# A two-layer graph network with experts on one Trainium2 core: three stages joined into one program per engine

## The chip, the cores and the metric

The kernel runs on one core of a Trainium2 chip. The metric is the device time of one execution in microseconds. Five instruction streams run beside each other: PE (TensorE), DVE (VectorE), ACT (ScalarE), POOL (GpSimd) and SP (SyncE), which here only issues DMAs. Streams wait for each other on semaphores. Gathers and scatters by an index (indirect DMAs) are issued by POOL alone.

## The reference, cut to what matters

12500 nodes of 256 numbers pass through four blocks, each added to x. All of them begin with a layer norm of x.

```python
x = x + L0_gnn(layernorm(x), edges)      # attention over 212500 edges, 4 heads
x = x + L0_ffn(layernorm(x))             # 8 experts of three layers, mixed by one softmax
x = x + L1_gnn(layernorm(x), edges)      # attention, 8 heads, then a layer norm with gains
x = x + L1_ffn(layernorm(x))             # this one has a router:
    # h = x @ W_gat (4 heads x 4 experts); attention over 131072 router edges gives scores
    # e = leaky_relu(a_src[src] + a_dst[dst]); softmax over the edges of one dst; agg = sum(alpha * h[src])
    # scores = layernorm(agg) averaged over heads; the top 2 of 4 experts, softmax over these two
    # out = sum over experts of gate * (gelu(x @ W1 + b1) @ W2 + b2)
```

The change is about the last two lines of x: the end of the second attention (L1_gnn), the experts of L1_ffn, and the attention over the router's edges.

## The kernel before, in words

Nodes stand in 98 blocks of 128 (node b * 128 + p on partition p). Everything is float32. The edges of both graphs are sorted by destination on the chip at the start. `gnn_two_layers` runs the stages one after another; each stage opens a `Ctx`, which holds its memory and semaphores, and a `Block` with one program for each engine. When a `Ctx` with semaphores closes, all engines meet at a barrier, the semaphores are cleared, and they meet again (L52).

The stages that matter here:

- **The message stage of the second attention** (`sum_messages`, tiles named g1sm). 1760 tiles of 128 edges, taken 32 at a time into two slots. POOL gathers the 128 source rows of a tile (L1276), DVE computes softmax weights and multiplies messages (L1529), PE adds the messages of one destination by a matrix of zeros and ones (L1384), DVE carries the running sums along (L1551), and SP writes them to `sums` in HBM. The gathers of a tile may start when PE has used the tile that stood in its place. At the start POOL issues 64 gathers, DVE prepares and waits for the first 32 of them by way of ACT (L1325) and PE (L1360).
- **The end of the second attention** (`finish_and_route`, tiles named g1fa). Blocks go in 49 pairs. POOL fetches the last running sum of each node of a pair (`Sums.fetch`, L1618, two indirect DMAs a pair, at most two pairs in flight), DVE divides by the sum of weights and takes part in two layer norms, ACT normalises and takes roots, PE transposes and multiplies by the router's weights. Results: the new x, the transposed normed rows `turned`, and the router's rows (24 numbers a node) in `keep`, which go to the table `rtab` in HBM. For each block POOL also scatters the destination's score to the first edge of each node in `rfill` (L1928). In POOL's program 24 pairs (`AHEAD`) are fetched first; then each pair n does the fetch of pair n + 24, if there is one, and the two scatters of pair n. At the end POOL waits until the table and all scatters are written.
- **The experts** (`expert_outputs`, tiles named f). 25 steps, 24 of four blocks and one of two. A step runs the four experts in turn: PE multiplies `turned` by W1 into four banks (L2590), ACT takes gelu (L2567), PE multiplies by W2 (L2607), DVE adds the bias (L2633), SP writes the output `z`. PE computes the hidden layer of the next expert before the outputs of the present one.
- **The sums over the router's edges** (`EdgeSums`, tiles named re), inside the experts' programs. Each partition has 1024 consecutive sorted edges; 22 groups of 46 and one of 12. `split_keys` (L748 to 785, 26 operations of DVE, each waiting for the one before) takes the sorted keys apart into source numbers (`src`), marks of a new destination (`first`) and what is needed to join the partitions. POOL's `fetch` (L799, L811) gathers one row of `rtab` for each edge column, 1024 in all, at most eight lots ahead of the experts' outputs. In step g + 3 DVE works on group g: `highs` (L846 to 865) after the second expert, `sums` (L876 to 885) after the fourth; ACT takes the exponents between them (L831), SP loads the scores of the destination (L819) and stores the rows to `rsum` (L825).
- **`finish`** (tiles named rf): group 22, and sums that go over the end of a partition are joined: two transposes on PE, short operations of DVE and ACT, one gather and one scatter on POOL.
- **`choose_and_sum`** (tiles named cs): the last stage.

Before the experts start there is a barrier at the end of `finish_and_route` and of the scope around it; then SP loads x and the keys, ACT copies the 98 x 24 node values to another place (L742), DVE splits the keys, and POOL waits for 18 of the 26 operations. Between the experts and `finish`, and after `finish`, there are barriers too.

Of the kernel before, what the change touches and what calls it, by code (L numbers as in the profile page):

```python
# [11 lines left out]
P = 128  # L12
# [20 lines left out]
HELD = 20  # L33
SPAN = 32
# [658 lines left out]
class EdgeSums:  # L693
# [4 lines left out]
    G, LAG = 46, 3  # L698

    def __init__(self, nc, K, c, cols, H, F, table, sorted_keys, start, count, nodes, made, fill, rsum, endi, has):  # L700
        self.nc, self.K, self.cols, self.H, self.table = nc, K, cols, H, table
        self.nodes, self.made = nodes, made
# [5 lines left out]
        assert self.REST > 0 and self.NG % 2 == 0  # L708
# [14 lines left out]
        (self.loaded, self.numbered, self.moved, self.ready, self.began_in, self.ad_in, self.piece, self.diff_ready,  # L723
         self.exp_ready, self.piece_done, self.kept) = (c.sem("re" + n) for n in (
             "loaded", "numbered", "moved", "ready", "began_in", "ad_in", "piece", "diff_ready", "exp_ready",
             "piece_done", "kept"))
        every = self.rows[:, :, :].rearrange("p c w -> p (c w)")
        spare = every[:, cols * X - 2 * (cols + 1):]
        self.dst, self.dstf = spare[:, 0:cols + 1].bitcast(I32), spare[:, cols + 1:2 * (cols + 1)]
        self.lone, self.run = spare[:, 0:cols], spare[:, cols + 1:2 * cols + 1]  # L730
        assert cols - -(-2 * (cols + 1) // X) >= 2 * self.G
# [13 lines left out]
    KEYS, SPLIT = 18, 26  # L745

    def split_keys(self, dve):
# [26 lines left out]
        assert link.n == self.KEYS  # L774
# [12 lines left out]

    def span(self, g):
        return (g * self.G, self.G if g < self.NG else self.REST)
# [3 lines left out]
    def fetch(self, pool, outputs):  # L793

        nc, G = self.nc, self.G
        nc.gpsimd.iota(self.base[:, :], [[0, 1]], base=0, channel_multiplier=self.cols).then_inc(self.numbered, 1)
        nc.gpsimd.iota(self.selfi[:, :], [[P, NB]], base=0, channel_multiplier=1).then_inc(self.numbered, 1)
        pool.wait_ge(self.ready, self.KEYS)
        nc.gpsimd.indirect_dma_start(self.began[:, :], None, self.table,  # L799
                                     bass.IndirectOffsetOnAxis(ap=self.head0[:, 0:1], axis=0)).then_inc(self.began_in, 16)  # L800
        for g in range(self.NG + 1):
            col, n = self.span(g)
            if g >= 2:
                pool.wait_ge(self.rows_in[g % 2], 16 * G * (g // 2))
            lots = [col + n * j // self.LOTS for j in range(self.LOTS)]
            for u in range(col, col + n):
# [4 lines left out]
                nc.gpsimd.indirect_dma_start(self.rows[:, u, :], None, self.table,  # L811
# [10 lines left out]
    def store(self, sp, g, col, n):  # L822

        sp.wait_ge(self.piece_done, g + 1)
        sp.dma_start(self.rsum.rearrange("(p c) w -> p c w", p=P)[:, bass.ds(col, n), :],  # L825
                     self.rows[:, bass.ds(col, n), :]).then_inc(self.kept, 16)
# [8 lines left out]
    def highs(self, dve, g, col, n, landed):  # L835
# [8 lines left out]
        high = lambda a, b: self.rows[:, bass.ds(col + a, b - a), W:X]  # L844
# [9 lines left out]
        link(tt(score, self.rows[:, bass.ds(col, n), 0:H], ad, ALU.add))  # L854
# [13 lines left out]
    def sums(self, dve, g, col, n):  # L868
# [5 lines left out]
        rows = lambda a, b, c, d: self.rows[:, bass.ds(col + a, b - a), c:d]  # L874
# [13 lines left out]
    def finish(self):  # L888
# [5 lines left out]
        with Ctx(nc, "rf") as c:  # L894
            turned = c.ps("turned", [P, 3, P])
            backp = c.ps("backp", [P, 2, W])
            wide = c.sb("wide", [P, 2, W])
            state = c.sb("state", [P, 3, P])
            high, total = c.sb("high", [P, P + 1]), c.sb("total", [P, P + 1])
            step = c.sb("step", [P, 2, P])  # L900
            met, join = c.sb("met", [P, X]), c.sb("join", [P, 3, W])
            merged = c.sb("merged", [P, X])
            (ch, spread, rows_turned, step_ready, step_exp, state_ready, back, met_in, join_ready, join_exp, merge_ready,
             merge_out) = (c.sem(q) for q in (
# [268 lines left out]
def sum_messages(nc, K, name, tiles, H, table, lay, sums, room, more, beside, landed, begun=0):  # L1173
# [10 lines left out]
    with Ctx(nc, name) as c:  # L1184
# [39 lines left out]
        with nc.Block() as block:  # L1224

            @block.sync
            def _(sp):
# [32 lines left out]
                if beside is not None:  # L1260
                    beside(sp)
# [1728 lines left out]
```

## Time and profile before

| | |
|---|---|
| median of 3 runs | 9239.54 us (9236.39 to 9247.44) |
| the profiled execution | 9238.97 us |
| its span, first to last instruction | 9237.2 us |
| busy in the span: PE, DVE, POOL, ACT | 75%, 69%, 56%, 36% |

A time in a row is counted in us from the start of the span. A row of a timeline has start, length, engine, line, operation, result and operands, and in brackets how long the engine was idle before it and what ended that. "issue" is idle time in which the engine waited for nothing that the profile shows; for POOL's indirect DMAs it is 0.3 us each. The rows of POOL's DMAs are the time that POOL works on the issue, not that of the transfer. A row of the table by stage has the stretch, its length, the busy time of PE, of its weight loads, of DVE, ACT and POOL with the number of instructions, the granted clock of PE as a share of 2.4 GHz, the share of the DMA engines, and GB/s.

### The profile page before, as it was taken

The page shows a single profiled execution, that of the slowest core. Times are in us where ns is not written, and L with a number is a line of the kernel's source. Part 1 is how long each engine was busy: PE and PEld are TensorE (multiplying, and loading weights), DVE is VectorE, ACT ScalarE, POOL GpSimd, SP SyncE. Part 2 cuts the span into 40 slices and gives each one's busy share as a digit, 9 for nine tenths or more (in the row PEclk, how much of TensorE's full clock was granted, in tenths as well). Part 3 has the DMA queues.
Part 4 walks back from the last instruction along what each step waited for, and adds up shares of the span by engine and source line. Part 5 has one row for each costly group of instructions (what it writes and reads, how often), then busy time and mean ns, then how long its engine had stood idle before and what let it go on. Part 6 is the DMA issues. An engine that isn't in the chain of part 4 may idle for free. (4 is left out here: it accounts for less than half of the span.)

```text
span 9237.2 us, 87312 instructions
## 1 busy us (share of the span) xinstructions
PE 6943.7 (75%) x21953; PEld 4016.8 (43%) x21953; DVE 6330.2 (69%) x18686; ACT 3346.2 (36%) x7429; POOL 5144.8 (56%) x5327
## 2 busy tenths in 40 slices
PE   1536666666668999999997677777777649999985
PEld 1422232222225555555555233333333346666665
DVE  9967777777778777787665788888888851322235
ACT  1324344434443333333334344444444452222224
POOL 0157777777771111011543777777777577777754
PEclk9868888888889999999998677777777659999997
DMA  3256776677661000000325677777677652222229
GB/s 121 68 164 219 223 222 217 219 222 223 217 220 54 28 28 28 19 28 31 27 24 161 201 224 225 220 225 226 219 224 225 207 173 54 73 71 69 67 64 340
DMA packets 672170, 1355.24 MB, mean 147 GB/s; under 512 B 203371, under 2 KB 401870, under 8 KB 670642
## 3 DMA queue, kind: packets, MB, share of 16 engines
q0 software_dynamic: 238688, 579.40, 24.2%
q1 hardware_dynamic: 406352, 744.60, 22.9%
q10 hardware_dynamic: 26626, 25.65, 0.8%
q8 instruction: 178, 2.92, 0.1%
q14 instruction: 326, 2.67, 0.1%
HBM read 712.31 MB, written 649.65 MB: 147 GB/s over the span
## 5 line engine op out<-in xcount | busy, mean ns | idle before, releaser
L1276 POOL DMA_INDIRECT g_acc<-htab,g1sm_src x1760 | 1687.6, 959 | 545.5 <-issue 495.0
L1276 POOL DMA_INDIRECT g_acc<-htab,g0sm_src x1740 | 1650.0, 948 | 541.7 <-issue 488.2
L1384 PE MATMUL g1sm_sump<-g_acc,g1sm_to 128*128 128x264 f32 x3520 | 1481.3, 530 | 355.1 <-DVE g_acc L1529 327.3
L1384 PE MATMUL g0sm_sump<-g_acc,g0sm_to 128*128 128x260 f32 x3520 | 1320.8, 476 | 268.6 <-DVE g_acc L1529 226.9
L811 POOL DMA_INDIRECT re_rerows<-rtab,re_resrc x1024 | 994.2, 971 | 312.1 <-issue 307.8
L1384 PEld LDWEIGHTS g1sm_sump<-g_acc,g1sm_to 128*128 128x128 f32 x3520 | 660.0, 233 | 1132.0 <-DVE g_acc L1529 778.1
L1384 PEld LDWEIGHTS g0sm_sump<-g_acc,g0sm_to 128*128 128x128 f32 x3520 | 593.7, 210 | 958.3 <-DVE g_acc L1529 649.7
L2213 POOL DMA_DIRECT2D x<-g_acc x25 | 20.0, 800 | 1490.6 <-DVEq L2448 1349.4
L2633 DVE TENSOR_TENSOR k_arena<-f_yp,k_arena 128x512 f32<-128x512 f32 x196 | 135.6, 692 | 966.7 <-PE f_yp L2607 966.7
L1529 DVE TENSOR_TENSOR g_acc<-g_acc,g1sm_weightp 128x256 f32<-128x256 f32 x1760 | 716.5, 407 | 67.1 <-ACT g1sm_weightp L1318 67.1
L1529 DVE TENSOR_TENSOR g_acc<-g_acc,g0sm_weightp 128x256 f32<-128x256 f32 x1760 | 717.6, 408 | 21.7 <-ACT g0sm_weightp L1318 21.7
L2344 PE MATMUL f_yp<-k_arena 128*128 128x256 f32 x3136 | 712.8, 380 | 12.9 <-DVE g_acc L2437 9.1
L2309 PE MATMUL f_h1p<-k_arena 128*128 128x512 f32 (+1 forms) x1600 | 708.6, 586 | 0.7 <-ACT k_arena L2265 0.7
L2309 PE MATMUL f_h2p<-k_arena 128*128 128x512 f32 (+1 forms) x1600 | 706.2, 584 | 0.9 <-ACT k_arena L2274 0.9
L2607 PE MATMUL f_yp<-k_arena 128*128 128x256 f32 x3136 | 693.3, 379 | 2.4 <-ACT k_arena L2567 2.4
L2344 PEld LDWEIGHTS f_yp<-k_arena 128*128 128x128 f32 x3136 | 594.4, 190 | 167.0 <-issue 79.4
L2437 DVE SCALAR_TENSOR_TENSOR g_acc<-f_yp,f_wgt,g_acc 128x256 f32<-128x256 f32 x784 | 342.5, 479 | 456.2 <-PE f_yp L2344 450.9
L2607 PEld LDWEIGHTS f_yp<-k_arena 128*128 128x128 f32 x3136 | 595.8, 190 | 124.3 <-issue 45.4
L2274 ACT ACTIVATE k_arena<-f_h2p,f_shift,f_scale 128x512 f32<-128x512 f32 (+1 forms) x400 | 304.6, 768 | 917.8 <-PE f_h2p L2309 917.8
L1305 ACT ACTIVATE g1sm_to<-k_iota,g1sm_side 128x128 f32<-128x128 f32 x1760 | 556.7, 386 | 116.7 <-PE g1sm_sump L1384 116.7
L1305 ACT ACTIVATE g0sm_to<-k_iota,g0sm_side 128x128 f32<-128x128 f32 x1760 | 556.8, 387 | 18.2 <-PE g0sm_sump L1384 17.3
L2567 ACT ACTIVATE k_arena<-f_hp,k_f1b1s 128x512 f32<-128x512 f32 (+1 forms) x400 | 264.3, 679 | 782.2 <-PE f_hp L2590 782.0
(462 smaller groups left out, 11199.1 us busy)
## 6 DMA issues: line engine op xcount, KB each, us to landing
sums<-k_arena SPq DMA_DIRECT2D x275, 528.0 KB
sums<-k_arena SPq DMA_DIRECT2D x220, 520.0 KB
sums<-g_acc SPq DMA_DIRECT2D x165, 528.0 KB, 4.4
sums<-g_acc SPq DMA_DIRECT2D x165, 520.0 KB, 4.2
z<-k_arena SPq DMA_DIRECT2D x96, 512.0 KB, 3.0
k_arena<-z SPq DMA_DIRECT2D x33, 1024.0 KB, 13.5
sums<-g0sm_now SPq DMA_DIRECT2D x55, 520.0 KB
g_acc<-htab,g1sm_src POOLq DMA_INDIRECT x1760
```

Of the source, the lines that this page charges most:

```text
L811: nc.gpsimd.indirect_dma_start(self.rows[:, u, :], None, self.table, bass.IndirectOffsetOnAxis(ap=self.src[:, u:u + 1], axis=0))\
L1276: nc.gpsimd.indirect_dma_start(slot[a][:, u, :], None, table, bass.IndirectOffsetOnAxis(ap=src[a][:, u:u + 1], axis=0)).then_inc(landed[a] ...
L1305: ab = nc.scalar.activation(to[s][:, u, :], K["iota"][:, :], ACT.Abs, bias=mark[a][:, q * LOT + u:q * LOT + u + 1])
L1384: nc.tensor.matmul(bank(k, u), to[u // LOT % RING][:, u % LOT, :], slot[a][:, u, 0:W], start=True, stop=True).then_inc(summed, 1)
L1529: tt(m, m, weight[:, u, :].unsqueeze(2).to_broadcast([P, H, D]), ALU.mult).then_inc(msg_ready, 1)
L2274: nc.scalar.activation(hs[e % 2][:, m, 0:J * P], pp[m][:, 0:J * P], ACT.Relu, bias=shift[:, l, e, m:m + 1], scale=scale[:, l, e, m:m + 1])\
L2309: mm = nc.tensor.matmul(pp[m][:, 0:J * P], ws[:, e, k, m * P:(m + 1) * P], rhs[:, k, 0:J * P], start=(k == 0), stop=(k == KC - 1))
L2344: mm = nc.tensor.matmul(yp[j // 2][:, j % 2, :], h2s[e % 2][:, k, j * P:(j + 1) * P], wos[:, e, k, :], start=(k == 0), stop=(k == KC - 1))
L2437: m = nc.vector.scalar_tensor_tensor(out=row, in0=yp[q][:, j % 2, :], scalar=wgt[:, j, e:e + 1], in1=row, op0=ALU.mult, op1=ALU.add)
L2567: nc.scalar.activation(hs[e % 2][:, m, 0:J * P], hp[m][:, 0:J * P], ACT.Gelu, bias=b1s[:, e, m:m + 1])\
L2607: mm = nc.tensor.matmul(yp[j // 2][:, j % 2, :], hs[e % 2][:, k, j * P:(j + 1) * P], w2s[:, e, k, :], start=(k == 0), stop=(k == HC - 1))
L2633: nc.vector.tensor_tensor(zs[e % 2][:, 2 * q:2 * q + 2, :], yp[q][:, :, :], b2s[:, e, :].unsqueeze(1).to_broadcast([P, 2, DIM]), ALU.add)\
```

## The change

The three programs of each engine (end of the attention, experts with the edges' sums, `finish`) are put one behind the other in a single `Block`; the barriers between them are gone, and semaphores order them. For this:

- `split_keys` and the load of its keys move to the start of the message stage (`sum_messages` has a new argument `keys`), on DVE ahead of the first tile's weights and on SP ahead of the load of the experts' weights; POOL's two iotas (`number`) stand ahead of its first gather.
- the running sums that are fetched keep 72 blocks instead of 80, and `AHEAD` is 36 pairs instead of 24.
- `keep` is now the place where the last stage reads the node values; ACT's copy is gone.
- the rows of the edges lie in the memory of the running sums, in a ring of ten groups; POOL waits for a group's store before the tenth group after it. Marks and source numbers lie in memory that the first layer's experts left.
- SP loads the experts' first rows of x halfway through the end of the attention. POOL no longer waits there for its scatters; SP does, after three steps of the experts. POOL waits for the table and for DVE's divisions, then gathers.
- PSUM is eight banks, shared by name: the transposes and the experts' outputs use banks 0 and 1, the router's products and `finish` 2 and 3, the hidden layers 4 to 7.

```diff
+KEPT = 72
-    G, LAG = 46, 3
+    G, LAG, RING = 46, 3, 10
...
-        self.src = c.sb("resrc", [P, cols], I32)
-        self.rows = c.sb("rerows", [P, cols, X])
-        self.first = c.sb("refirst", [P, cols])
+        self.src, self.first = marks[:, 0:cols].bitcast(I32), marks[:, cols:2 * cols]
+        self.rows = room[:, 0:self.RING * self.G * X].rearrange("p (c w) -> p c w", w=X)
...
-    def keep_nodes(self, act):
-        self.nc.scalar.copy(self.nodes, self.made).then_inc(self.moved, 1)
-        act.wait_ge(self.moved, 1)
+    def number(self, pool):
+        nc = self.nc
+        nc.gpsimd.iota(self.base[:, :], [[0, 1]], base=0, channel_multiplier=self.cols).then_inc(self.numbered, 1)
+        nc.gpsimd.iota(self.selfi[:, :], [[P, NB]], base=0, channel_multiplier=1).then_inc(self.numbered, 1)
...
+    def held(self, g):
+        return g % self.RING * self.G
...
     def fetch(self, pool, outputs):
-        nc.gpsimd.iota(self.base[:, :], [[0, 1]], base=0, channel_multiplier=self.cols).then_inc(self.numbered, 1)
-        nc.gpsimd.iota(self.selfi[:, :], [[P, NB]], base=0, channel_multiplier=1).then_inc(self.numbered, 1)
-        pool.wait_ge(self.ready, self.KEYS)
         nc.gpsimd.indirect_dma_start(self.began[:, :], None, self.table,
...
             if g >= 2:
                 pool.wait_ge(self.rows_in[g % 2], 16 * G * (g // 2))
+            if g >= self.RING:
+                pool.wait_ge(self.kept, 16 * (g - self.RING + 1))
...
-                nc.gpsimd.indirect_dma_start(self.rows[:, u, :], None, self.table,
+                nc.gpsimd.indirect_dma_start(self.rows[:, self.held(g) + u - col, :], None, self.table,
...
-def sum_messages(nc, K, name, tiles, H, table, lay, sums, room, more, beside, landed, begun=0):
+def sum_messages(nc, K, name, tiles, H, table, lay, sums, room, more, beside, landed, begun=0, keys=None):
...
-                if beside is not None:
-                    beside(sp)
+                if keys is not None:
+                    keys.load_keys(sp)
+                beside(sp)
...
+                if keys is not None:
+                    keys.number(pool)
...
                 dve.wait_ge(cleared, 3)
+                if keys is not None:
+                    keys.split_keys(dve)
                 for s in range(HEAD):
                     weigh(s, 0, 0, 0)
...
-    N, R, AHEAD, LATE, TURNED = NB // 2, 4, 24, 8, 7
+    N, R, LATE, TURNED = NB // 2, 4, 8, 7
-    KEPT = HELD * CHUNK // 2
+    PAIRS = AHEAD = KEPT // 2
...
+            if n == N // 2:
+                for q in range(CHUNK // 2):
+                    sp.wait_ge(xT_kept[q], 16)
+                ahead(sp)
         for s in range(R):
             sp.wait_ge(xT_kept[s], 16 * len(range(s, N, R)))
+        sp.wait_ge(done, N)
...
         pool.wait_ge(kept, 16 * N)
-        pool.wait_ge(placed, 16 * NB)
+        pool.wait_ge(divided, N)
...
         for i in range(LAG):
             step(i, CHUNK, CHUNK)
+        sp.wait_ge(placed, 16 * NB)
         edges.load(sp, 0, 0, G)
...
-                edges.keep_nodes(act)
-                edges.split_keys(dve)
...
-            acc = g.sb("acc", [P, HELD * CHUNK, DIM + heads[1]])
+                places = g.sb("acc", [P, KEPT * width])[:, :]
...
+                with nc.Block() as block:
+                    @block.gpsimd
+                    def _(pool):
+                        fa_pool(pool)
+                        ex_pool(pool)
+                        rf_pool(pool)
+                    @block.tensor
+                    def _(pe):
+                        fa_pe(pe)
+                        ex_pe(pe)
+                        rf_pe(pe)
+                    @block.vector
+                    def _(dve):
+                        fa_dve(dve)
+                        ex_dve(dve)
+                        rf_dve(dve)
...
```

SP and ACT are joined in the same way. What each engine computes is unchanged.

## Rows read from the trace of the kernel before

**Rows 1.** Table by stage: end of attention, seam, experts; columns as told above.
```profile
7407.00:7545.00 138.00, 74.99 (x340) 71.50 (x340) 103.14 (x437) 86.31 (x222) 108.12 (x99) 0.50 0.75 217
7571.00:7621.00 50.00, 0.14 (x1) 0.04 (x2) 0.14 (x2) 2.35 (x2) 27.00 (x30) 0.50 0.08 20
7621.00:8940.00 1319.00, 1318.98 (x4580) 871.31 (x4581) 356.20 (x1032) 322.91 (x448) 994.71 (x1025) 1.00 0.27 67
```

**Rows 2.** Groups by line: POOL's gathers of messages; busy, mean, idle before them.
```profile
L1276 POOL DMA_INDIRECT g_acc<-htab,g1sm_src x1760 | 1687.6, 959 | 545.5 <-issue 495.0 <-PE g1sm_sump L1384 40.8 <-DMA g1sm_src<-srcs 9.6
```

**Rows 3.** Waits in the experts' stage: us in total, times, longest.
```profile
POOL re_rerows L811 <- issue: 307.8, 1010, 0.3
```

**Rows 4.** Timeline, first expert matmul of PE and first edge gather of POOL.
```profile
7621.02 16.79 PE L2590 MATMUL f_hp<-k_arena 128*128 128x512 f32 x32 [49.87 <-DMA k_arena<-turned]
...
7634.53 0.96 POOL L811 DMA_INDIRECT re_rerows<-rtab,re_resrc  x1 [0.30 <-issue]
```

**Rows 5.** Timeline of POOL, end of the attention: fetches (L1618) and scatters (L1928).
```profile
7327.12 0.98 POOL L1618 DMA_INDIRECT g_acc<-sums,k_lasts  x1 [56.01 <-POOLq L52]
...
7366.49 1.01 POOL L1618 DMA_INDIRECT g_acc<-sums,k_lasts  x1 [1.30 <-DMA g_acc<-sums,k_lasts]
...
7406.66 1.29 POOL L1928 DMA_INDIRECT rfill<-k_arena,k_starti  x1 [0.31 <-issue]
...
7539.94 1.19 POOL L1618 DMA_INDIRECT g_acc<-sums,k_lasts  x1 [0.30 <-issue]
...
7604.95 0.98 POOL L1928 DMA_INDIRECT rfill<-k_arena,k_starti  x1 [0.30 <-issue]
```

**Rows 6.** Timeline of DVE, end of the attention: divisions 13 and 29, last reciprocal.
```profile
7377.23 0.69 DVE L2027 TENSOR_TENSOR g1fa_t<-g_acc,g1fa_rden 128x512 f32<-128x512 f32 x1
...
7437.15 0.69 DVE L2027 TENSOR_TENSOR g1fa_t<-g_acc,g1fa_rden 128x512 f32<-128x512 f32 x1
...
7545.02 0.25 DVE L2020 RECIPROCAL g1fa_rden<-g_acc 128x16 f32<-128x16 f32 x1 [3.93 <-DMA g_acc<-sums,k_lasts]
```

**Rows 7.** Timeline, start of the message stage: gathers 1 and 32, first use.
```profile
5047.65 1.02 POOL L1276 DMA_INDIRECT g_acc<-htab,g1sm_src  x1 [9.60 <-DMA g1sm_src<-srcs]
...
5086.52 0.95 POOL L1276 DMA_INDIRECT g_acc<-htab,g1sm_src  x1 [0.30 <-issue]
...
5089.32 1.05 ACT L1325 COPY g1sm_asrc<-g_acc 128x512 f32<-128x512 f32 x1 [56.24 <-DMA g_acc<-htab,g1sm_src]
...
5091.58 0.49 DVE L1433 SCALAR_TENSOR_TENSOR g1sm_fill<-g1sm_ends,g1sm_smallp 128x128 f32<-128x128 f32 x2 [40.20 <-PE g1sm_smallp L1360]
```

**Rows 8.** Timeline of DVE, the split of the keys: first, eighth, last long operation.
```profile
7623.54 0.69 DVE L756 TENSOR_SCALAR re_resrc<-re_rerows 128x1024 int32<-128x1024 int32 x1 [6.62 <-DMA re_rerows<-rsorted]
...
7630.23 1.22 DVE L764 TENSOR_REDUCE re_relead<-re_rerows 128x1 f32<-128x1024 f32 x1
...
7635.17 0.36 DVE L785 CAST r_endi<-re_retmpn 128x98 int32<-128x98 f32 x1
```

**Rows 9.** Timeline in the edges' layout, early on: a gather beside a wide operation.
```profile
528.23 2.28 DVE L1125 SCALAR_TENSOR_TENSOR k_arena<-k_arena 128x2048 f32<-128x2048 f32 x1
528.66 2.74 POOL L1053 DMA_INDIRECT g_acc<-htab,el_srcs  x1 [11.68 <-DVE el_srcs L1106]
```

**Rows 10.** Timeline at the end: group 21's last gather, first use, join, last stage.
```profile
8924.21 0.94 POOL L811 DMA_INDIRECT re_rerows<-rtab,re_resrc  x1 [0.30 <-issue]
...
8965.83 0.35 DVE L854 TENSOR_TENSOR re_rediff<-re_rerows,re_read 128x184 f32<-128x184 f32 x1
...
8985.59 0.17 DVE L846 TENSOR_SCALAR re_relow<-re_refirst 128x12 f32<-128x12 f32 x1 [2.13 <-PEq L52]
...
9006.86 0.34 SPq L2699 DMA_DIRECT2D cs_par<-in_L_ffn_b_gat_dram  x1
```

**Rows 11.** Table by stage: the experts' first microseconds, columns as in rows 1.
```profile
7621.00:7624.00 3.00, 2.98 (x4) 1.45 (x5) 0.46 (x1) 0.00 (x0) 0.00 (x0) 0.50 0.68 210
7627.00:7630.00 3.00, 3.00 (x9) 1.33 (x8) 2.93 (x3) 1.37 (x2) 0.00 (x0) 1.00 0.00 0
```

More of the change, by code:

```diff
@@ new lines, in finish, with sync @@
+        wide, join = parts[4].rearrange("p (q w) -> p q w", q=2), parts[6].rearrange("p (q w) -> p q w", q=3)
+        (ch, spread, rows_turned, step_ready, step_exp, state_ready, back, met_in, join_ready, join_exp, merge_ready,
+         merge_out) = (c.sem("rf" + q) for q in (
+             "ch", "spread", "rows_turned", "step_ready", "step_exp", "state_ready", "back", "met_in", "join_ready",
+             "join_exp", "merge_ready", "merge_out"))
+        def sync(sp):
+            self.store(sp, NG, col, n)
@@ new lines, in scalar, with tensor @@
+        def scalar(act):
+            self.weigh(act, NG, n)
+            act.wait_ge(step_ready, 1)
+            nc.scalar.activation(step[0:W, :, :], step[0:W, :, :], ACT.Exp).then_inc(step_exp, 1)
+            act.wait_ge(join_ready, 1)
+            nc.scalar.activation(join[:, 0:2, :], join[:, 0:2, :], ACT.Exp).then_inc(join_exp, 1)
+        def tensor(pe):
+            pe.wait_ge(spread, 1)
+            for q, t in enumerate((self.edge[:, 0:W], wide[:, 0, :], wide[:, 1, :])):
+                mm = nc.tensor.transpose(turned[0:W, q, :], t, K["ident"][:, :])
+            mm.then_inc(rows_turned, 1)
+            pe.wait_ge(state_ready, 1)
+            for q, t in enumerate((total, high)):
+                mm = nc.tensor.transpose(backp[:, q, :], t[0:W, 0:P], K["ident"][0:W, 0:W])
+            mm.then_inc(back, 1)
@@ L1842, in _, with finish_and_route @@
                     pool.wait_ge(stored[s], 16 * len(range(s, N, HS)))
-def finish_and_route(nc, K, name, acc, H, xin, xout, gamma, ws, table, keep, arena, sums, start, count, fill, starti, turned):
+def finish_and_route(nc, K, c, banks, acc, H, xin, xout, gamma, ws, table, keep, arena, sums, start, count, fill, starti, turned,
+                     ahead, placed):
     D = DIM // H
-    N, R, AHEAD, LATE, TURNED = NB // 2, 4, 24, 8, 7
+    N, R, LATE, TURNED = NB // 2, 4, 8, 7
     C, TW = ws.shape[2], table.shape[1]
@@ new lines, in gpsimd, with scalar, step @@
+    def gpsimd(pool):
+        assert edges.LOTS == 2 * NE and (edges.NG + 1) * edges.LOTS - 1 - edges.AHEAD <= (NCH - 1) * 2 * NE + LAST // 2 * NE
+        edges.fetch(pool, y_ready)
+    def scalar(act):
+        def step(i, J, g=None):
+            for e in range(NE):
+                for m in range(HC):
+                    act.wait_ge(h_ready, i * (NE * HC) + e * HC + m + 1)
+                    nc.scalar.activation(hs[e % 2][:, m, 0:J * P], hp[m][:, 0:J * P], ACT.Gelu,
+                                         bias=b1s[:, e, m:m + 1])\
+                      .then_inc(h_done, 1)
+                if e == 2 and g is not None:
+                    edges.weigh(act, g, edges.G)
+        act.wait_ge(w_in, 16 * w["loads"])
+        for i in range(edges.LAG):
+            step(i, CHUNK)
+        for g in range(0, edges.NG - 1):
+            step(g + edges.LAG, CHUNK, g)
+        step(NCH - 1, LAST, edges.NG - 1)
```

869 lines of the change are left out of this document (411 added, 458 removed).

## Prediction

> **What bounds the kernel now.** I read the table by stage first, then the groups by line and the waits, then timelines around the two seams that the change closes. The end of the second attention runs from 7326 to 7571, and its table rows show PE at a granted clock of 0.50, the 1.2 GHz level, and POOL and DVE busy most of the time; then comes a stretch of 50 us in which PE does nothing and POOL works 27 us; then 1319 us of experts with PE busy throughout at 1.00, the 2.4 GHz level [rows 1]. So the experts look bound by PE, and the seam before them looks like a gift. The second look spoils this. In the message stage POOL's 1760 gathers take 1687.6 us, and of the 545.5 us between them 495.0 are "issue": POOL never waits for anybody [rows 2]. In the experts it is the same: before 1010 of the 1024 gathers the idle time is an issue gap of 0.3 us, 307.8 us in all [rows 3], so POOL runs from 7634.53 to about 8940 without a stop, at 1.27 us a gather, and ends only some 37 us before the last expert result. Two engines stand almost level here. The reader should see that PE can be started 74 us earlier, and that this is worth only what POOL can follow.
>
> At the seam PE waits 49.87 us, until 7621.02, for its first rows of x; POOL starts its gathers at 7634.53, as it waits for the split of the keys [rows 4]. In the end of the attention POOL issues 98 fetches and 98 scatters of 1.25 to 1.7 us each, from 7327.12 to 7606 [rows 5], 279 us: POOL is the longest chain there too. The scatters after the last fetch hold nobody but the barrier.
>
> **Message stage: the split moves in.** The 26 chained operations of the split took DVE from 7623.54 to 7635.5, 12 us [rows 8]. They now stand where DVE sat 40.20 us until 5091.58, waiting for PE, which waits for the first 32 gathers (the last issued at 5086.52, its data used at 5089.32, 2.8 us later) [rows 7]. The key load on SP's queue stands ahead of the expert weights, which nobody needs for 2 ms. A load that lands by 5060 has the split done by 5072, so DVE's time is hidden; without that cover it would be 12 us. POOL's two iotas fit ahead of its first gather, at 5047.65, while it waits for the indices. What isn't hidden is what the split does to the gathers: POOL never waits here, so each us taken from it comes back at the end of the stage. The nearest row: a gather issued during a 2.28 us vector operation between SBUF operands lasted 2.74 us in place of some 0.95 [rows 9]. Six such wide operations stand from 7623.54 to 7630.23 [rows 8], 6.7 us. Bounds: nothing, and 6.7 us if POOL stands still throughout; I take 3.5.
>
> A rule of the Trainium skill speaks against this edit: "SBUF — State Buffer", section "A bandwidth-pool intuition that's wrong", says that a two-port vector operation locks GpSimd out, so that it can't write descriptors until the operation ends. The row agrees [rows 9]; by the rule alone the cost is the upper end, 6.7 us, and the forecast would be 3.2 us later.
>
> **End of the attention: 36 pairs ahead in place of 24.** With 24, POOL issues 50 fetches, from 7327.12 to 7406.66, before the first scatter (79.5 us); the last 24 of them, from 7366.49, took 40.2 us [rows 5]. With 36 it issues 74. Then come rounds of two fetches and two scatters. Before: from 7406.66 two scatters (2.6 us), 23 rounds, and the second fetch 1.4 us into the 24th at 7539.94, so 5.62 us a round. Then 50 scatters up to 7604.95, 1.30 each [rows 5]. After:
>
> 7327.1 + 3.5 (split) + 79.5 + 40.2 + 2.6 = 7453.0; 12 rounds, 67.4, to 7520.4; 72 scatters, 93.6, to 7614.0.
>
> So POOL itself ends 8 us later than now, but all else is earlier. The last fetch is issued at 7453.0 + 11 x 5.62 + 1.4 = 7516.2 in place of 7539.94. Its data came 5.1 us later (the reciprocal at 7545.02), and PE's last matmul of the stage ended 26.1 us after that, at 7571.15 (7621.02 less 49.87) [rows 4 to 6]. That gives 7547.4. DVE can follow: 16 pairs from 7377.23 to 7437.15 are 3.75 us a pair, where POOL was ahead [rows 6]; 36 more pairs from the 13th end at 7515.6 with the split's 3.5, before the data of the last fetch.
>
> **No barrier before the experts.** PE's program goes on with its first expert matmul. Its x was loaded halfway through the stage, its weights long ago; the semaphore that opens the hidden banks is given by DVE when its part ends, before PE's. ACT first waits for its last stores of x, issued some 10 us earlier. So PE starts at 7547.4 in place of 7621.02: 73.6 us earlier. The copy of the nodes (2.15 us of ACT) goes; it ran while PE waited, worth nothing by itself.
>
> **POOL.** Its wait for the scatters to land, the barriers and the wait for the split go; after 7614.0 stands one gather of 1.3 us, so the first gather of rows is at 7615.3 in place of 7634.53: 19.2 us earlier. Its new wait, for the store of the group ten back, has some six steps of margin. The wait for the scatters is now SP's, after three expert steps, some 160 us after PE's start (7707), where the scatters are done at 7614; behind it are SP's loads and stores of results, and it costs nothing unless scatters run 90 us late.
>
> **The end.** The last full group's gathers end with the issue at 8924.21, and DVE first used them at 8965.83, 39 us after they landed [rows 10]. Now PE's side moves by 73.6, to 8892.2, and POOL's by 19.2: issue at 8905.0, landing 2.8 us later [rows 7] at 8907.8. POOL ends last, by 15.6 us. From there the chain to the last stage is as before, 41.0 us to 9006.86 [rows 10]: DVE's maxima, ACT's exponents, the last two experts, the sums, the joining of the partitions. So the last stage starts 58.0 us earlier. The exit before the join showed as 2.13 us [rows 10], but the load of the next scores runs in that time; of the two exits at the very end one goes, which no row shows alone. Between nothing and 2.1; I take 1.
>
> Sum: 59.0 us. The profiled span was 9237.2 us and its execution 9238.97; the median shown is 9239.54, so the two differ by a half us. Predicted: 9180.5.
>
> **Rivals.**
> PE sets the end. If the deeper look-ahead brings nothing, PE ends the attention at 7571.15 + 3.5 and starts 46.4 us earlier; DVE would ask at 8919.4, after POOL's 8907.8: 47.4 gained, 9192. For it: the fetches waited for their own landing, which a longer run of them keeps. Against it: DVE already worked at its own pace while fetches were ahead [rows 6].
> POOL loses less. No lock in the split (3.5), and rounds at four times 1.30 rather than 5.62 (5 us): 67.5 gained, 9172.
> POOL loses more. The split costs 6.7, and scatters beside the experts and busier DVE cost 5 to 10 more: 44 to 51 gained, 9189 to 9196. For it: [rows 9].
> The seam stays. Some engine of the joined program waits for the scatters before experts can run: PE starts at 7617, and 5 us are gained: 9235, no change. I find no such wait but SP's.
> Slower: the clock. PE now goes straight from 245 us at 0.50 into the experts. If it stayed there, a step would take twice its time. PE has 15.6 us to spare, so 75 us of delay, or 150 us of experts at 1.2 GHz, eat the gain; beyond that it is slower, by some 1260 us if the whole stage of 1319 us doubled. Against it: after the seam the clock read 0.50 in the first 3 us of experts and 1.00 from 7627 [rows 11], with nothing but dense matmuls in between; and the rate before the seam was 0.50 too.
>
> **Chances.** The forecast, POOL-bound within 8 us: 0.58. PE sets the end: 0.14. POOL loses more: 0.14. Loses less: 0.08. The seam stays: 0.03. Clock, or another stall: 0.03. The range 9166 to 9197 takes in the POOL bounds and the case of PE, and leaves the last two and the tails. A fifth of a per cent, 18 us, is about what a measurement of this kernel tells from nothing: faster 0.94, no change 0.03, slower 0.03.
>
> **What would show it.** First expert matmul near 7547 with no long wait before it; first gather of edge rows near 7615; all gathers in one unbroken row; a wait of DVE of some 15 us for gathered rows in the last expert step, with PE idle there, the only one of its kind; the last stage starting near 8948. Long gathers (1.5 us and more) between 5058 and 5072 show the lock, and the message stage then ends 2 to 6 us later. The prediction is wrong if PE starts late, if the clock stays at 0.50, or if gathers beside the experts' start take more than 1.3 us.

## The result and the profile after

The changed kernel takes 9194.69 us (median of 5 runs, 9187.19 to 9195.98) against 9239.54 (5 runs, 9233.94 to 9247.44): a ratio of 0.9949, interval 0.9935 to 0.9963. The gain is 44.9 us where 59.0 were forecast. In the profiled executions the span falls from 9237.2 to 9194.1, by 43.1; the sums below are made against these two. The profiled execution after the change is the slowest of its five.

The table by stage (columns as in [rows 1]) shows the seam closed. The 50 us in which PE did nothing are experts at full clock, and PE is busy without a break from 7551 to 8894. The rival of the clock stayed away: the granted clock read 0.51, near the 1.2 GHz level, in the first 5 us of the experts, and 1.00 behind them. New is the stretch from 8900 to 8920, in which PE stands idle:

```profile
7551.40:7556.40 5.00, 5.00 (x7) 2.16 (x8) 0.00 (x0) 1.34 (x2) 3.78 (x5) 0.51 0.39 112
7556.40:7561.00 4.60, 4.60 (x12) 2.09 (x11) 0.00 (x0) 2.24 (x5) 3.38 (x5) 1.00 0.02 1
7571.00:7621.00 50.00, 50.00 (x174) 32.74 (x173) 5.54 (x8) 9.62 (x14) 38.15 (x39) 1.00 0.15 43
7551.00:8894.00 1343.00, 1343.00 (x4694) 892.68 (x4695) 353.43 (x1034) 330.09 (x462) 1022.77 (x1052) 1.00 0.27 67
8900.00:8920.00 20.00, 0.47 (x3) 0.07 (x1) 3.90 (x13) 3.31 (x6) 15.13 (x17) 0.61 0.14 22
8920.00:8926.00 6.00, 5.90 (x16) 4.67 (x16) 0.00 (x0) 1.33 (x2) 4.50 (x5) 0.58 0.11 10
```

The timeline of PE and POOL at the seam answers to [rows 4, 5]: the first scatter, PE's first expert matmul (it has no wait ahead of it), the last scatter, and the first gather of rows, 2.6 us behind it.

```profile
7453.83 1.30 POOL L1932 DMA_INDIRECT rfill<-r_nodes,k_starti  x1 [0.30 <-issue]
...
7551.39 16.40 PE L2587 MATMUL g_bank<-k_ws,k_arena 128*128 128x512 f32 x32
...
7617.63 0.98 POOL L1932 DMA_INDIRECT rfill<-r_nodes,k_starti  x1 [0.30 <-issue]
...
7620.21 0.97 POOL L809 DMA_INDIRECT g_acc<-rtab,k_f0bos  x1 [0.30 <-issue]
```

The waits of POOL in the experts, as in [rows 3]: still only issue gaps, and 20 short ones that end with a matmul.

```profile
POOL g_acc L809 <- issue: 305.9, 1004, 0.3
POOL g_acc L809 <- PE g_bank L2604: 6.1, 20, 0.3
```

The timeline at the end answers to [rows 10]. DVE waits 17.30 us for the rows of group 21, PE waits 19.63 us for ACT, which weighs that group first; then come a wait of 2.75 us for the next scores, the merging scatter, and the last stage.

```profile
8913.09 0.35 DVE L853 TENSOR_TENSOR g_rediff<-g_acc,g_read 128x184 f32<-128x184 f32 x1 [17.30 <-DMA g_acc<-rtab,k_f0bos]
...
8920.10 6.13 PE L2604 MATMUL g_bank<-k_arena 128*128 128x256 f32 x16 [19.63 <-ACT k_arena L2566]
...
8936.27 0.69 DVE L850 TENSOR_TENSOR_SCAN g_read<-g_reinner,g_rebegan,g_read 128x12 f32<-128x12 f32 x4 [2.75 <-DMA g_read<-rfill]
...
8951.80 1.01 POOL L934 DMA_INDIRECT rsum<-g_x,g_regoali  x1 [4.93 <-DVEq L978]
...
8964.30 0.34 SPq L2696 DMA_DIRECT2D cs_par<-in_L_ffn_b_gat_dram  x1
```

Group 21 is used 52.7 us earlier than before, the last stage starts only 42.6 us earlier. So 10.2 us are lost behind the point where POOL stops being the bound: from the first use to the merging scatter it takes 38.71 us (before 36.30), and from there to the last stage 12.50 us. Before, that was 4.73 us, from this row to the last of [rows 10]:

```profile
9002.13 1.03 POOL L939 DMA_INDIRECT rsum<-rf_merged,re_regoali  x1 [4.93 <-DVEq L984]
```

What POOL's sequencer does in those 12.50 us stands in the view of one source line (operation, count, shortest/median/longest ns, start): a DRAIN, the instruction with which each engine's program ends here, 8.71 us long (the exit, below, is this end of a program with the barrier behind it). It starts when the scatter has landed, for which POOL's program waits.

```profile
L2960 POOLq DRAIN  x1: 8710/8710/8710, 8954.1 to 8954.1; - x1
```

The kernel before has one such DRAIN behind each of its three programs here: the attention's end, the experts, the join.

```profile
L1889 POOLq DRAIN  x1: 7077/7077/7077, 7607.3 to 7607.3; - x1
L2517 POOLq DRAIN  x1: 23844/23844/23844, 8925.2 to 8925.2; - x1
L907 POOLq DRAIN  x1: 217/217/217, 9004.5 to 9004.5; - x1
```

The second stands in POOL's queue from 8925.2 and ends at 8949.0, 8.6 us behind the last gather; nobody waited for it, since PE and DVE worked on for 35 us. The third, two transfers later, takes 0.22 us. Before the change the join had its long DRAIN paid out of sight. Joined with the experts, the join has that long DRAIN on the path.

### The profile page after: what moved, and what is told of

Same layout as the page of the kernel before. It is cut to its first block and busy times, and to the rows that moved or that the text cites. A ratio compares the mean times of both kernels' runs of the same rounds, so it can differ in the third digit from the quotient of the medians.

```text
span 9194.1 us, 87195 instructions
## 1 busy us (share of the span) xinstructions
PE 6943.8 (76%) x21953; PEld 4017.2 (44%) x21953; DVE 6327.9 (69%) x18686; ACT 3343.6 (36%) x7428; POOL 5148.5 (56%) x5327
## 3 DMA queue, kind: packets, MB, share of 16 engines
q14 instruction: 325, 2.66, 0.1%
## 5 line engine op out<-in xcount | busy, mean ns | idle before, releaser
L809 POOL DMA_INDIRECT g_acc<-rtab,k_f0bos x1024 | 995.1, 972 | 312.0 <-issue 305.9
L2629 DVE TENSOR_TENSOR k_arena<-g_bank,k_arena 128x512 f32<-128x512 f32 x196 | 135.6, 692 | 991.0 <-PE g_bank L2604 990.6
L1528 DVE TENSOR_TENSOR g_acc<-g_acc,g0sm_weightp 128x256 f32<-128x256 f32 x1760 | 711.8, 405 | 21.7 <-ACT g0sm_weightp L1317 21.7
L2347 PE MATMUL f_yp<-k_arena 128*128 128x256 f32 x3136 | 712.5, 380 | 11.3 <-DVE g_acc L2440 7.6
L1550 DVE SCALAR_TENSOR_TENSOR k_arena<-k_arena,g1sm_side,g1sm_sump 128x264 f32<-128x264 f32 x1485 | 711.8, 479 | 0.3
L2604 PE MATMUL g_bank<-k_arena 128*128 128x256 f32 x3136 | 695.7, 380 | 19.6 <-ACT k_arena L2566 19.6
L2347 PEld LDWEIGHTS f_yp<-k_arena 128*128 128x128 f32 x3136 | 594.5, 190 | 164.9 <-issue 79.4
L2604 PEld LDWEIGHTS g_bank<-k_arena 128*128 128x128 f32 x3136 | 597.5, 191 | 142.2 <-issue 45.4
```

Source lines behind the costliest of these rows:

```text
L809: nc.gpsimd.indirect_dma_start(self.rows[:, self.held(g) + u - col, :], None, self.table, bass.IndirectOffsetOnAxis(ap=self.src[:, u:u + 1 ...
L1528: tt(m, m, weight[:, u, :].unsqueeze(2).to_broadcast([P, H, D]), ALU.mult).then_inc(msg_ready, 1)
L1550: stt(out=row(u), in0=before, scalar=keep[a][:, u:u + 1], in1=bank(k, u), op0=ALU.mult, op1=ALU.add).then_inc(added, 1)
L2347: mm = nc.tensor.matmul(yp[j // 2][:, j % 2, :], h2s[e % 2][:, k, j * P:(j + 1) * P], wos[:, e, k, :], start=(k == 0), stop=(k == KC - 1))
L2604: mm = nc.tensor.matmul(yp[j // 2][:, j % 2, :], hs[e % 2][:, k, j * P:(j + 1) * P], w2s[:, e, k, :], start=(k == 0), stop=(k == HC - 1))
L2629: nc.vector.tensor_tensor(zs[e % 2][:, 2 * q:2 * q + 2, :], yp[q][:, :, :], b2s[:, e, :].unsqueeze(1).to_broadcast([P, 2, DIM]), ALU.add)\
```

## The experiments

The start of the attention's end moves by up to 9 us between profiled executions (7324.9 to 7334.5). So times that are compared are counted from POOL's first fetch there. Each of e1 to e7 was executed once, and several of their times lie within what the five runs of the kernel after differ by (9187.19 to 9195.98); what they show is read from waits and starts inside the executions, and not from the totals. The table is worked out from the timelines, in us: first fetch; then, counted from it, PE's first expert matmul, POOL's first gather of rows, the start of the last stage; and the span.

```
kernel            fetch     PE    POOL    last     span
before           7327.1  293.9   307.4  1679.7   9237.2
after            7331.1  220.3   289.1  1633.2   9194.1
e1_drain_early   7333.0  215.6   285.6  1622.9   9187.0
e2_ahead24       7325.4  237.5   275.4  1631.5   9186.5
e3_ahead30       7327.8  225.7   279.0  1624.4   9182.5
e4_split_later   7334.5  220.2   287.7  1632.3   9196.0
e5_last_step     7328.9  219.0   289.0  1626.9   9186.2
e6_seam_back     7329.2  294.4   296.2  1688.1   9246.7
e7_drain_seam    7326.0  216.5   294.0  1641.2   9197.0
e8_combined      7327.7  225.1   278.4  1614.1   9172.4
e9_sums_first    7324.9  230.8   284.1  1615.1   9169.2
e10_ahead27      7327.0  236.7   281.0  1615.0   9171.8
```

Four kernels with 36 pairs and the same program up to POOL's first gather of rows (after, e1, e5, and e7 without its DRAIN of 7.5) stand between 285.6 and 289.1 there, so a difference of 3 or 4 us in that column tells nothing. From the start of the last stage to the end of the span it is 229.2 to 231.1 us in all twelve.

**The DRAIN at the exit.**

```
         def gpsimd(pool):
+            nc.gpsimd.drain()
             pool.wait_ge(self.kept, 16 * (NG + 1))
```

> The kernel after the change, with one more DRAIN of POOL right behind its last gather of rows, ahead of its wait for the stored sums. In the kernel after, the DRAIN that ends the joined program lasts 8.71 us and starts when the last scatter has landed. Theory: the length is left over from the long run of POOL's own transfers (the DRAIN behind the experts of the kernel before ended 8.6 us after the last gather, out of sight, and the one behind its join, with two transfers since, lasted 0.22). Then the new DRAIN ends some 8.6 us after the last gather, about 10 us before POOL is wanted again; the one at the exit falls from 8.71 to 0.2 to 0.5; from the merging scatter to the last stage it is 4 in place of 12.5 us, and the span falls by 8 to 8.5 us from 9194.1, to about 9186. Rival: the length belongs to the joined program's exit itself (its size, or the scatter just ahead of it): the exit's DRAIN stays near 8.7 and the span stays within 1 us of 9194.

The view by source line shows the new DRAIN and the one at the exit, the timeline the start of the last stage:

```profile
L929 POOLq DRAIN  x1: 23612/23612/23612, 8911.4 to 8911.4; - x1
...
L2961 POOLq DRAIN  x1: 222/222/222, 8954.1 to 8954.1; - x1
```

```profile
8951.79 1.02 POOL L935 DMA_INDIRECT rsum<-g_x,g_regoali  x1 [4.95 <-DVEq L979]
...
8955.84 0.34 SPq L2697 DMA_DIRECT2D cs_par<-in_L_ffn_b_gat_dram  x1
```

The early DRAIN ends at 8935.0, 8.6 us behind the last gather and 10.8 us before POOL is wanted. The exit's is 0.22, and the scatter, at the same time as in the kernel after, is followed by the last stage after 4.05 us: 8.45 us won. The rival, that the length belongs to the joined program's exit, is out.

> The kernel after the change with one more DRAIN of POOL ahead of its first gather of rows, behind the scatters of the attention's end. Theory, the length is left over from transfers since the last DRAIN: the new one holds POOL 7 to 8.7 us, the 1024 gathers behind it make the one at the exit long again, 8.7 us, and as POOL sets the end, the span is 7 to 9 us longer, 9201 to 9203. Rival, one early DRAIN pays for all, or the length grows with everything since the stage's start: the exit's falls to 0.2 or to well below 8, and the span stays near 9194.

This kernel has the same added line ahead of the gather of the rows where the groups begin, L795 in the kernel after. Its timeline and source view:

```profile
7609.92 0.98 POOL L1933 DMA_INDIRECT rfill<-r_nodes,k_starti  x1 [0.30 <-issue]
7618.74 0.98 POOL L796 DMA_INDIRECT g_rebegan<-rtab,g_rehead  x1 [7.84 <-issue]
```

```profile
L2961 POOLq DRAIN  x1: 8715/8715/8715, 8957.0 to 8957.0; - x1
```

POOL stands 7.5 us longer behind its scatters than the usual 0.3, and the exit's DRAIN is as long as ever. The last stage starts 8.0 us later on the count of the table; the span itself, 9197.0, is below the 9201 to 9203 expected, since this execution entered the stage 5.1 us earlier. So the length comes from what was transferred since the last DRAIN, and not in proportion: 98 fetches and 98 scatters leave 7, 1024 gathers leave 8.6, two leave 0.2. And 7.5 us put on POOL alone come back in full at the end, which says that POOL is the bound.

**How far ahead.** 24 pairs in e2, 30 in e3, where the kernel after has 36; the room for 36 stays.

```
-    PAIRS = AHEAD = KEPT // 2
+    PAIRS, AHEAD = KEPT // 2, 24
```

> The kernel after the change with 24 pairs fetched ahead, as before the change, and nothing else. Theory, POOL sets the end: POOL's first gather of rows comes 8.7 us earlier (7611.5), as scatters fill the waits of the fetches; PE's first expert matmul comes 21.7 us later (7573). PE's reserve in the last step is 17.3 us, so this goes 13 us too far: DVE's wait for group 21 vanishes, PE bounds the end, group 21 is used 4.4 us later than in the kernel after, PE's slow last expert gets 2.5 us back, and the span is 9195 to 9199. Rival, PE's start sets the end: all of the 21.7 us, span 9216. Second rival, POOL's start alone sets the end: span 9185.

> The kernel after the change with 30 pairs fetched ahead. Theory, POOL sets the end by 17.3 us: PE starts 10.9 us later (7562), POOL 3.5 to 4.5 us earlier (7616), PE's reserve shrinks to some 2.5 us and the span falls by 3.5 to 6.5 us, to 9188 to 9191 (the upper gain if PE's clock no longer falls in a wait of 20 us). Rival, PE's start sets the end: 10.9 us more, 9205.

First use of group 21 in the timelines, with 24 and with 30 pairs:

```profile
8906.36 0.35 DVE L853 TENSOR_TENSOR g_rediff<-g_acc,g_read 128x184 f32<-128x184 f32 x1
```

```profile
8900.61 0.35 DVE L853 TENSOR_TENSOR g_rediff<-g_acc,g_read 128x184 f32<-128x184 f32 x1 [2.75 <-DMA g_acc<-rtab,k_f0bos]
```

With 24 PE starts 17.2 us later and POOL 13.7 earlier than in the kernel after; DVE no longer waits, and PE bounds the end, as expected; but group 21 is used 1.0 us sooner on the table's count, where 4.4 later was expected, and the last stage comes 1.7 us sooner, too little to tell from nothing. With 30 it is 5.4 and 10.1, DVE still waits 2.75, and the last stage comes 8.8 us sooner. Both rivals that let one engine alone set the end are out: PE's start alone would have made both slower, POOL's start alone would have made 24 the fastest. Both theories had the mechanism and missed the sizes: with 24 and 30 pairs POOL gained 13.7 and 10.1 us where 8.7 and about 4 were reckoned, and PE lost 17.2 and 5.4 where 21.7 and 10.9 were. Both point one way: the deep look-ahead costs POOL more than reckoned. The waits of POOL in the attention's end show why, with 36 and with 24 pairs (us in total, times, longest):

```profile
POOL g_acc L1619 <- DMA g_acc<-sums,k_lasts: 29.7, 26, 3.4
```

```profile
POOL g_acc L1619 <- DMA g_acc<-sums,k_lasts: 17.2, 19, 1.7
```

A long run of fetches waits for its own landings; with scatters between them that time is used. The 12.5 us between the two rows are most of the 13.7.

The expectation for 30 pairs left open whether PE's clock would still fall in a shorter wait. It did: behind a wait of 5.09 us the last 16 matmuls took 6.56 us, and the granted clock read 0.50, the 1.2 GHz level, from 8908 to 8912.

```profile
8907.63 6.56 PE L2604 MATMUL g_bank<-k_arena 128*128 128x256 f32 x16 [5.09 <-ACT k_arena L2566]
```

**The split of the keys**, from the message stage to the head of DVE's part in the joined program.

```
-                if keys is not None:
-                    keys.split_keys(dve)
...
+                        edges.split_keys(dve)
                         fa_dve(dve)
```

> The kernel after the change, with the 26 operations of the key split moved out of the message stage to the head of DVE's part in the end of the second attention; the load of the keys stays where it is. In the kernel after and in four variants of it the first 32 gathers of the message stage took 42.4 to 43.3 us against 40.12 before the change. Theory, a gather beside a wide vector operation waits for that operation's end: the first 32 gathers take 40.1 again, and the fetches of the attention's end that run beside the split get 2 to 3 us longer instead; POOL's first gather of rows moves by less than 1.5 us against the stage's start, PE's first expert matmul by 5 to 12 us later (DVE starts 12 us late), inside PE's reserve of 17.3 us: the span stays within 3 us of 9194. Rival, the long gathers come from the load of the keys beside them: they stay in the message stage (42 to 43 us), and nothing else gets longer.

In the kernel after, the timeline of the message stage shows the gathers stretched beside the split:

```profile
5057.07 1.24 POOL L1273 DMA_INDIRECT g_acc<-htab,g1sm_src  x1 [0.30 <-issue]
...
5060.26 1.68 POOL L1273 DMA_INDIRECT g_acc<-htab,g1sm_src  x1 [0.30 <-issue]
...
5061.86 2.29 DVE L760 TENSOR_TENSOR_SCAN r_nodes<-r_nodes 128x1024 f32<-128x1024 f32 x1
5062.25 2.66 POOL L1273 DMA_INDIRECT g_acc<-htab,g1sm_src  x1 [0.30 <-issue]
5064.19 1.22 DVE L761 TENSOR_REDUCE g_relead<-r_nodes 128x1 f32<-128x1024 f32 x1
...
5065.21 0.95 POOL L1273 DMA_INDIRECT g_acc<-htab,g1sm_src  x1 [0.30 <-issue]
```

With the split moved, the same is seen in the other stage:

```profile
7338.56 2.29 DVE L760 TENSOR_TENSOR_SCAN r_nodes<-r_nodes 128x1024 f32<-128x1024 f32 x1
...
7338.95 2.65 POOL L1617 DMA_INDIRECT g_acc<-sums,k_lasts  x1 [0.30 <-issue]
```

The first 32 gathers take 40.18 us again, in place of 42.4 to 43.3, with the load of the keys still beside them. So it is the split, and it follows it. PE's start does not come 5 to 12 us later: it is where it was (220.2). DVE's waits took the split up; those for the fetched sums fell from 24.0 to 12.5 us. The span, 9196.0, is no better: the stretch moves from one part of POOL's chain to another.

**The barrier at the seam.** The joined program is split in two behind the end of the attention, for each engine as for POOL here; all else stays.

```
                 with nc.Block() as block:
...
+                    block.gpsimd(fa_pool)
...
+                with nc.Block() as block:
...
                     @block.gpsimd
                     def _(pool):
-                        fa_pool(pool)
                         ex_pool(pool)
                         rf_pool(pool)
```

> The kernel after the change with one barrier put back: the end of the attention is a program of its own, and experts and join are the second one; 36 pairs ahead, the moved split and the ring of 10 groups stay. Theory: POOL's DRAIN behind its scatters takes 7 to 9 us, so PE and POOL both start at about 7628 (PE 77 us later than in the kernel after, POOL 8 to 9 us later); PE bounds the end by far, group 21 is used near 8972, the exit's DRAIN stays 8.7, and the span is 9247 to 9253, slower than the kernel before (9237). Rival, POOL's start is all that counts at this seam: span 9202 to 9204.

```profile
7623.56 3.75 PE L2587 MATMUL g_bank<-k_ws,k_arena 128*128 128x512 f32 x4 [75.78 <-DVEq L2618]
```

PE waits 75.78 us and starts where it did in the kernel before (294.4 against 293.9), POOL 7.1 us later than in the kernel after; group 21 is used at 8968.25. The span is 9246.7, just under the 9247 to 9253 expected: all that the change won is lost, and 9.5 more, of which 7.8 is the exit's long DRAIN. POOL's start alone would have given 9202 to 9204, so that rival is out. The start of PE at the seam is what the change is worth.

**The last step, and all together.** e5 takes the edge work of group 21 out of the last expert step and puts it behind it, on ACT as here and on DVE alike:

```
-        step(NCH - 1, LAST, edges.NG - 1)
+        step(NCH - 1, LAST)
+        edges.weigh(act, edges.NG - 1, edges.G)
```

> The kernel after the change with the edge work of group 21 (maxima and sums on DVE, exponents on ACT) behind the last expert step in place of between its experts, in each engine's order. Theory, the gathers of POOL set the end and the experts of the last step only wait behind them in ACT's and DVE's order: PE's wait of 19.6 us for ACT vanishes and its last expert ends near 8904; group 21 is still used first at 8913; its sums follow at 8918 in place of 8927.2; group 22 starts with its gathers, near 8929, in place of 8936.3; so the merging scatter is 7 us earlier (8944.8) and the span near 9187. The DRAIN at the exit stays 8.7. Rival: the wait for the last expert is not on the path (stores of its results or the load of the next scores end last): less than 2 us, span 9192 to 9195.

```profile
8928.50 0.21 DVE L853 TENSOR_TENSOR g_rediff<-g_acc,g_read 128x48 f32<-128x48 f32 x1 [1.91 <-DMA g_acc<-rtab,k_f0bos]
```

Group 22 waits for its own gathers, and starts 6.3 us earlier on the table's count than in the kernel after. PE's wait of 19.6 us is gone, and the last stage starts the same 6.3 us sooner, where 7 were expected: the last expert did wait behind POOL, by the order in which ACT works.

> The kernel after the change with three edits together: POOL's DRAIN right behind its last gather, 30 pairs ahead in place of 36, and group 21's edge work behind the last expert step. Alone they gave spans of 9187.0, 9182.5 and 9186.2 against 9194.1. Theory: the 30 pairs make POOL's gathers end some 9 to 10 us sooner against the stage's start; the changed order lets group 22 start 2.5 us behind its last gather; the early DRAIN takes 8.5 us from the exit. With all three the last scatter comes near 8931, the last stage starts at 8935, span 9161 to 9169. Rival: the 30 pairs and the changed order pay for the same wait of PE, and only one of them counts: span 9172 to 9177.

9176.89 us in 5 runs, ratio to the kernel before 0.9936 (0.9922 to 0.9949); the span is 9172.4. The rival was right: with 30 pairs POOL is no longer late, and to move group 21 behind the experts then puts it behind PE (first use at 8909.08, with no wait for rows, where e3 had it at 8900.61).

Two more kernels keep the early DRAIN and 30 or 27 pairs, leave the maxima in their place, and let the sums of group 21 go ahead of the last addition (`at` is 2 in the last step, 3 in the others):

```
-                if e == 3 and g is not None:
+                if e == at and g is not None:
                     edges.sums(dve, g, g * G, G)
```

> The kernel after the change with POOL's DRAIN right behind its last gather, 30 pairs ahead, and a smaller change of order than in the combined run: in the last expert step only the sums of group 21 stand before the last expert's addition on DVE (not behind it), and SP stores them and loads the next scores before the last expert's result. Theory: in the combined run group 22 waited for group 21's maxima, which stood behind the last addition (8907 to 8913), and for scores that SP loaded late (2.76 us); here the maxima follow their gathers (8901), the sums end near 8911, and group 22 starts with its own gathers, 2.5 us behind the last one, near 8916 in place of 8923.0; the last stage starts near 8935 in place of 8941.9, span 9164 to 9168, the median of the runs some 7 us below that of the combined run. Rival: the experts' results (PE, the stores of SP) are what ends last; then it stays within 2 us of the combined run's 9172.4.

> The same kernel with 27 pairs ahead in place of 30. Theory: POOL's last gather comes 1.5 to 3 us sooner against the stage's start, PE some 5 us later; group 22 still waits for its own gathers, so the last stage starts 1 to 3 us sooner (against the stage's start; the stage's start itself moves by some 3 us from run to run). Rival: PE is the bound here already: 3 to 5 us later than with 30.

```profile
8921.18 0.21 DVE L853 TENSOR_TENSOR g_rediff<-g_acc,g_read 128x48 f32<-128x48 f32 x1 [1.43 <-DMA g_acc<-rtab,k_f0bos]
```

```profile
8922.41 0.69 DVE L850 TENSOR_TENSOR_SCAN g_read<-g_reinner,g_rebegan,g_read 128x12 f32<-128x12 f32 x4 [1.07 <-DMA g_read<-rfill]
```

The first row is from e9, with 30 pairs, the second from e10, with 27. With 30 group 22 waits for its gathers, as expected, but POOL's last gather came 7.6 us later on the table's count than in the combined run with the same 30 (its first 5.7 later already; why is not shown), so nothing was won over it (1615.1 against 1614.1), where 7 us were expected. That is the size which the rival had, but not its cause, as the experts' results are not what group 22 waits for. With 27 POOL's last gather comes 3.5 us sooner and PE 5.9 us later, group 22 waits for the scores instead, and the last stage starts where it did with 30 (1615.0): neither the 1 to 3 us sooner of the theory nor the 3 to 5 later of the rival. The two engines stand level and the rest is below what can be told apart. The runs: 9175.09 us (0.9927, 0.9914 to 0.9941) with 30, 9172.22 (0.9926, 0.9912 to 0.9939) with 27. These are the fastest medians of all, some 20 us below the kernel after by the medians, about twice the spread of the runs of each, though the intervals of the ratios still touch (0.9935 and up for the kernel after).

## Why the prediction was right, and where its size was off

The time is inside the stated range, and the mechanism was the one forecast. But 9194.7 is 14.2 us above the forecast of 9180.5, outside the 8 us of its own case; that it fell inside the range is owed to the room left for other rivals, so in that part it is luck.

**The mechanism.** POOL bounds the end, PE stands ready and waits: DVE's wait in the last step is 17.30 us where 15.6 were forecast, with PE idle, the only one of its kind. e2, e3 and e7 show that POOL is the bound and how far; e6 shows that PE's earlier start is where the gain comes from.

**The split.** Forecast 3.5 us between 0 and 6.7; the first 32 gathers took 3.16 us longer, 2.2 to 3.2 in the kernels that kept it there. The Trainium skill ("SBUF — State Buffer", "A bandwidth-pool intuition that's wrong") says that GpSimd can't write a DMA's descriptors until the two-port vector operation beside it ends. The rows of the stretched gathers agree: the one of 2.66 us ends 0.76 us behind the scan, the three others each 0.12 us behind an operation of 0.69 us. The sum by that rule alone, 6.7, was too high: POOL still got four gathers done in that time, which take 5.0 us without the split and took 8.1. And not every wide operation counts: the gather of 2.66 us ended while the reduction of 1.22 us (L761) was still running, and the next one, begun in its last 0.2 us, took 0.95 as ever. POOL's next stage began 4.0 us later; what is left above the split's share lies inside what gathers 33 to 1760 differ by from one execution to the next (2180.1 to 2185.2 us).

**POOL in the attention's end.** First scatter forecast at 7450.3, measured 7453.83; first gather of rows 7615.3 and 7620.21; first use of group 21 at 8907.8 and 8913.09. So POOL's gain is 52.7 in place of 58.0: the term of the fetches ahead was 3 us short, since a longer run of fetches waits longer for its own landings, 0.5 is the message stage, and the rounds of fetches and scatters make up most of the rest. PE's start, 7547.4 and 7551.39, was 4 us late for the same reason, at no cost.

**The step that failed** is the one behind it: "From there the chain to the last stage is as before, 41.0 us". It measured 51.2. The prediction copied the old chain, took the exits as a price that can only fall, and counted one exit less as a gain of 1 us. But the join's exit was cheap before because the experts' exit, just ahead, had taken POOL's long DRAIN behind other engines' work. Of the 10.2 us, 7.8 are the DRAIN: 12.50 us from the scatter to the last stage in place of 4.73. The other 2.4 are the last 16 matmuls of PE, which took 6.13 us at a granted clock of 0.58 after the idle stretch, in place of 3.72. That the exit of 2.13 us ahead of the join went gained nothing, as the prediction had said: before, DVE waited these 2.13 us and 0.76 more for the scores, now it waits 2.75 for them, and from its last copy of group 21 (L884) to the scan of the scores it is 3.3 us in both kernels.

```profile
8986.60 0.69 DVE L851 TENSOR_TENSOR_SCAN re_read<-re_reinner,re_rebegan,re_read 128x12 f32<-128x12 f32 x4 [0.76 <-DMA re_read<-rfill]
```

From the last stage to the end of the span it is 0.5 us less than before, where 1 was taken for the exit that goes. That is less than what this stretch differs by from one execution to the next, so no run shows that term.

The sum in the forecast's terms: -59.0 + 5.3 (POOL) + 2.4 + 7.8 (chain) + 0.4 (end) = -43.1. The measured 9194.7 lies where the rival "POOL loses more" had its times, but not by its cause: POOL's gain fell short by 5.3, within the 8 us of the forecast's own case, and the rest came from behind POOL.

What stays open: why a DRAIN behind a long run of POOL's transfers takes 7 to 8.7 us when their data has landed; that it does, and that it can be paid early, is shown. Open too is why POOL's gathers began 5.7 us later in e9 than in the combined run.

## What to carry to other kernels

When two programs are joined, list what each exit did besides the barrier, for each engine's sequencer, and ask which other work it was hidden behind; in the joined program it may stand on the path. An engine that never waits can be the next bound even where another one is busy throughout at full clock, so weigh a deeper look-ahead by what it costs that engine: in the changed kernel 36 pairs were too many and 24 too few. Where two engines stand almost level, edits that each win alone need not add up: here 8.5, 8.8 and 6.3 us alone, 19.1 together.

## What the runs showed of the hardware

POOL's DRAIN is not a constant: 0.22 us two transfers behind another DRAIN, 7.1 behind 196 indirect transfers, 8.6 to 8.7 behind 1024, where those of 7.1 and 8.7 began after the data had landed. A DRAIN given earlier, in a wait of POOL, takes this off the exit.

In the kernel after, the granted clock read 1.00 until PE fell idle at 8900.5 and 0.50, the 1.2 GHz level, from 8910 to 8920, and the 16 matmuls behind this wait took 6.13 us at 0.58, where 16 such matmuls take 3.62 at 1.00. Shorter waits were followed by the same: the 16 took 6.56 us behind a wait of 5.09 (e3), 6.57 behind 5.67 (e9) and 5.41 behind 2.38 (e10), while a wait of 2.38 in the kernel before was followed by 3.72 at 1.00. What tells these last two apart is not shown.

Beside DVE's scan of 2.29 us a gather of POOL took 2.66 us in place of 0.95, and ended while the reduction of 1.22 us that followed was still running.
